# Attention beside routed experts on one core: the output bias in eight group additions ahead of the returns, and a small memset behind each return

## What is computed

```
xn  = layernorm(x)
att = linear attention with 16 heads and exp features(xn) @ w_out + b_out
gates = sinkhorn((xn @ router_w.T + router_b) / temperature), 3 iterations
top 2 experts of 8 for each token, their gates normalised
y   = sum over the 2 experts of gate * ((relu(xn @ wg) * (xn @ wp)) @ wo)
out = x + att + (xn + y)
```

## Time and profile before

| | |
|---|---|
| runs | 329.74 us median of 3 (328.19 to 330.65) |
| profiled execution | 327.3 us, its span 325.5 us |
| busy share of the span | PE 84%, DVE 68%, ACT 49%, POOL 73% |
| mean granted TensorE clock | 0.909 of full speed |
| scatter on POOL | until 164.9 us |
| return on POOL | 177.6 to 301.3 us |
| combination and stores | from 302.3 us to the end |

### The profile page before, as it was taken

How to read it: one execution, slowest core, us unless ns; L and a number is a source line. 1 busy time by engine, 2 the same in 40 slices (tenths; PEclk the granted TensorE clock), 3 DMA queues, 4 the chain that set the end, 5 groups by cost and what they waited for, 6 DMA issues and landing times.

```text
span 325.5 us, 6627 instructions
## 1 busy us (share of the span) xinstructions
PE 274.7 (84%) x2044; PEld 257.5 (79%) x2044; DVE 222.9 (68%) x523; ACT 160.3 (49%) x365; POOL 237.6 (73%) x388
## 2 busy tenths in 40 slices
PE   5996878799999999999699999999999999850020
PEld 4896777689999999999599999999999999850010
DVE  4948889668888778888855777777777774500173
ACT  2774562134555555455346677777777775210000
POOL 5899520757888888888611688888888888888381
PEclk9998996589999999999979999999999999885555
DMA  7974000551111111111142598898888841111694
GB/s 236 339 272 164 4 0 0 167 191 45 47 50 52 45 49 46 47 50 51 36 110 61 166 244 245 244 256 251 245 246 248 251 134 48 42 49 40 226 383 174
DMA packets 32462, 45.22 MB, mean 139 GB/s; under 512 B 5328, under 2 KB 21200, under 8 KB 32432
## 3 DMA queue, kind: packets, MB, share of 16 engines
q1 hardware_dynamic: 26592, 33.83, 34.1%
q0 software_dynamic: 4544, 9.84, 9.0%
q10 hardware_dynamic: 1296, 1.20, 1.1%
HBM read 27.17 MB, written 17.68 MB: 138 GB/s over the span
## 4 chain that ended last, share of the span: by engine, by line
PE 49%; POOL 23%; DVE 12%; DMA 6%; issue 5%; ACT 2%; SPq 1%; ACTq 0%; POOLq 0%; DVEq 0%
POOL rows_y L541 17%; PE bank L642 7%; PE bank L666 6%; POOL acc L496 5%; PE bank L618 4%; PE bank L619 4%; PE bank L620 4%; PE bank L656 4%; PE bank L795 3%; DMA xn<-rows_y 2%; PE bank L591 2%; PE bank L783 2%; PE bank L574 2%; PE bank L784 2%; PE bank L785 2%
## 5 line engine op out<-in xcount | busy, mean ns | idle before, releaser
L541 POOL DMA_INDIRECT rows_y<-xn,row_i x78 | 80.5, 1032 | 28.2 <-ACT xn L969 15.1
L532 POOL DMA_INDIRECT slots_x<-xn,slot_i x64 | 63.9, 999 | 29.4 <-DVE slot_i L1195 10.1
L871 ACT ACTIVATE feat<-z_sb 128x512 f32<-128x512 f32 x64 | 39.9, 631 | 65.7 <-DVE z_sb L1065 65.7
L1058 DVE TENSOR_REDUCE neg_max<-bank 128x16 f32<-128x512 f32 x64 | 42.7, 684 | 19.8 <-PE bank L620 19.8
L783 PE MATMUL bank<-xT_high,w_high 128*128 128x256 f32 x156 | 47.3, 303 | 0.5 <-issue 0.5
L785 PE MATMUL bank<-xT_high,w_low 128*128 128x256 f32 x156 | 44.0, 282 | 0.0
L784 PE MATMUL bank<-xT_low,w_high 128*128 128x256 f32 x156 | 44.0, 282 | 0.0
L1065 DVE TENSOR_TENSOR z_sb<-bank,neg_max 128x512 f32<-128x512 f32 x64 | 42.6, 684 | 0.5
L795 PE MATMUL bank<-w_tile,hidden 128*128 128x128 f32 x312 | 41.0, 275 | 0.0
L642 PEld LDWEIGHTS bank<-v_aug,feat 128*128 128x128 f32 x256 | 31.5, 200 | 8.8 <-issue 7.4
L795 PEld LDWEIGHTS bank<-w_tile,hidden 128*128 128x128 f32 x312 | 38.2, 192 | 0.1
(11 more groups left out here) (145 smaller groups left out, 562.5 us busy)
## 6 DMA issues: line engine op xcount, KB each, us to landing
w_tile<-w_expert_dram SPq DMA_DIRECT2D x39, 384.0 KB
slots_x<-w_tile SPq DMA_DIRECT2D x39, 144.0 KB, 2.2
x_tile<-slots_x SPq DMA_DIRECT2D x39, 130.0 KB
acc<-x_dram SPq DMA_DIRECT2D x8, 256.0 KB, 5.3
xn<-rows_y SPq DMA_DIRECT2D x8, 256.0 KB, 5.8
w_tile<-rows_y SPq DMA_DIRECT2D x8, 256.0 KB, 6.5
rows_y<-xn,row_i POOLq DMA_INDIRECT x78, 3.7
slots_x<-xn,slot_i POOLq DMA_INDIRECT x64, 2.3
```

The costliest lines, as they stand in the source:

```text
L532: pool.indirect_dma_start(slots_x, bass.IndirectOffsetOnAxis(slot_i[k][:, i:i + 1], 0), xn[:, j, :], None).then_inc(scattered[n % FLIGHT], 16)
L541: pool.indirect_dma_start(rows_y, bass.IndirectOffsetOnAxis(row_i[:, k, t:t + 1], 0), y_tile(k, t), None)\
L871: act.activation(feat[par][n][:, :], z_sb[n][:, :], ACT.Exp).then_inc(feat_ready, 1)
L1058: dve.tensor_reduce(neg_max[n][:, :], args(n), AX_X, ALU.max, negate=True).then_inc(z_negmax, 1)
```

## The change

`add_bias` now takes a whole group of four tiles (128 x 512 elements) in one POOL instruction, with the bias repeated over the four tiles. The eight of them stand between the last scatter and the first return. Group g waits until the projections of its tiles are in `acc`, for groups 6 and 7 until 13 projections are. In `send_rows` there is no addition any more; behind each of the 78 return DMAs stands a memset of one column of `gap`, which is twice as wide now. DVE waits once for all eight groups, ahead of `add_projection(13)`; its later waits for the bias are gone. The depths of the expert pipeline (`LOOP`, `UP`, `YR`) stay as they are.

```
-        gap = sb("gap", [P, SLOT_TILES])
+        gap = sb("gap", [P, 2 * SLOT_TILES])
...
-            def add_bias(n):
-
-                j, cols = half_tile((n + 4 * (EARLY - 1)) % (2 * NT))
-                pool.tensor_tensor(acc[:, j, cols], acc[:, j, cols], b_out_sb[:, cols], ALU.add).then_inc(bias_added, 1)
+            def add_bias(g):
+
+                tiles = acc[:, g * GROUP:(g + 1) * GROUP, :]
+                pool.tensor_tensor(tiles, tiles, over_tiles(b_out_sb, GROUP), ALU.add).then_inc(bias_added, 1)
...
                 for t in range(2):
                     pool.indirect_dma_start(rows_y, bass.IndirectOffsetOnAxis(row_i[:, k, t:t + 1], 0), y_tile(k, t), None)\
                         .then_inc(y_sent[k % YR], 16)
-                    n = 2 * k + t
-                    for piece in range(n * NT // SLOT_TILES, (n + 1) * NT // SLOT_TILES):
-                        add_bias(piece)
-                pool.memset(gap[:, k:k + 1], 0.0)
+                    pool.memset(gap[:, 2 * k + t:2 * k + t + 1], 0.0)
 
             pool.wait_ge(base_added, 2 * NT)
+            for g in range(NG):
+                pool.wait_ge(acc_added, min(GROUP // 2 * (g + 1), EARLY - 1))
+                add_bias(g)
             pool.wait_ge(acc_added, EARLY - 1)
             for k in range(SLOT_TILES):
                 send_rows(k)
 
-            pool.wait_ge(bias_added, 2 * NT)
+            pool.wait_ge(bias_added, NG)
...
                 dve.wait_ge(base_added, 4 * b + 4)
-                if late(b, EARLY - 1):
-                    dve.wait_ge(bias_added, 2 * NT - 4 * (EARLY - 1))
+                if b == EARLY - 1:
+                    dve.wait_ge(bias_added, NG)
...
                 step(b, b // 2, b % 2, front=b + 1 < NB)
-            dve.wait_ge(bias_added, 2 * NT)
             combine_group(0)
```

## The result

The changed kernel took 335.75 us (median of 4 runs, 332.7 to 337.32), the kernel before 328.97 beside it (327.89 to 330.65). The ratio is 1.019, 95% interval 1.010 to 1.0281: slower, by something between 1% and 3%, where I had forecast 312 us and a range up to 320. The profiled execution took 337.32 us, its span 335.5.

A forecast was written before the change was run, and what follows sets the result against it. POOL's returns were taken as the bound: from 182.41, 96.75 of distances and 2.6 of collisions, plus 0.3 and 25.55 to the end, gave 307.65, taken as 308.0; with run overheads 312 us, range 308 to 320.

The forecast's parts named there:

- What bounded the kernel: End of the chain: 84 us in a row on POOL's returns, each microsecond off coming off the end until DVE's 287.8.
- The additions and memsets: POOL's return: without additions 75 distances of 1.29 us make 96.75; 39 new memsets cost nothing, 4.3 us if uncovered.
- Collisions: POOL's returns held up by DVE's `w_low`: 6.1 us before, taken as 2.6 after, between 0 and 6.1.
- the second rival: Returns lock onto DVE's `w_low`: 15 us of collisions in place of 2.6, 324 us; chance 8%.
- The group additions: Eight on POOL before the first return: 12 us hidden in 12.74 idle; disturbing DVE's `row_i` costs 0.3, bounds 0 to 1.3.
- The rule on the shared port: Whoever starts first holds the port for the whole instruction; DVE's wait beside group additions could be 1.26 to 1.4 us.
- What is late next: Expert loop with faster returns: about 8 GB/s more DMA traffic, little room for row loads, so the loop may end later.
- x: How much later the expert loop ends: taken as 2 us, between 0 and 6.
- the sum: End of kernel: 307.65 by POOL, 307.64 by DVE, taken as 308.0 for the span, 17.5 us below 325.5.
- the landing of the row loads: Expert loop: landing 0.4 us or more longer makes loads the pace, loop 6 to 10 us later, up to 320; 12%.
- The rival "slower": Expert loop: row loads land after over 5.5 us in place of 4.5, loop 25 us later, 335 us; chance 4%.

The follow-up runs named there:

- third group: On one chip beside the kernel before: changed kernel unedited 305.88 us, with one memset a return pair 304.77, with a 128 x 256 memset behind each return 321.23.
- fast chips: Chips on which the changed kernel and its close relatives took some 306 us, where others gave 332 to 337 us.
- first group: Changed kernel with an addition behind each return 331.27 us, a wide memset instead 321.81, one memset a pair 306.07; kernel before with a memset behind every return 326.59.
- fourth group: Changed kernel unedited 306.1 us; with 128 x 256 memsets behind each return 321.83, a third of weights loaded 305.01, two such memsets behind each pair 342.93.
- slow kind: Chips, or jobs, in which the changed kernel and its close relatives took 332 to 337 us in place of some 306.
- two slow jobs: The result's job (changed kernel, 335.75 us) and a job of four edits to its return memsets (none, one a pair, counted, 128 wide), 331.79 to 336.47 us.
- the bare one: Changed kernel with no memset at all in the return: 336.47 us in one job, 306.05 us in another.

## Why the prediction was wrong

**What bounded the kernel: right.** The 84 us on POOL were the bound, and where nothing else goes wrong each microsecond off the return comes off the end, within a microsecond or two (the table). With the changed kernel this has come to its limit, as forecast: there DVE's late attention ends no earlier than the first plane lands.

**The additions and memsets: right.** The changed kernel on the chip of the third group needs 97.0 us from its second pair (183.33) to its last return (280.36); the forecast was 96.75 + 2.6 = 99.4. 70 of its 75 distances are 1.26 to 1.28 us, where I took 1.29; that is most of the difference. A memset behind every return costs nothing: with it, with one a pair and with none the time is 305.9, 306.1 or 304.8, and 306.1 on the fast chips.

**Collisions: fewer than taken.** One return there takes longer than the others, 1.28 us, and their mean is 0.965. The other four of the five longer distances (1.37 to 2.01 us) hold no long return. All five together give 1.9 us, against the 2.6 that I allowed. And in the kernel before it is 11 returns that take 1.22 to 1.47 us, not the 12 that I counted; they give 3.8 us. What the prediction says of them holds in each case: all 11 start while DVE's `w_low` runs and end 0.86 us after it ends. The lock that the second rival feared was seen as well, though not in the changed kernel: with the addition behind each return (first group) 9 returns in a row, one in every second slot tile from 220.9 to 261.5 us, start just behind the start of a `w_low` and take 1.48 to 1.50 us.

```profile
L541 POOL DMA_INDIRECT rows_y<-xn,row_i x78 | 75.3, 965 | 22.7 <-issue 15.7
```

**The group additions: hidden, as forecast,** 9.93 us in a gap of 12.7 where I took 12. The effect on DVE was there: the first two `row_i` take 0.62 and 0.99 us beside them, 0.15 otherwise:

```profile
172.83 0.62 DVE L1274 TENSOR_TENSOR row_i<-x_tile,spare_row 128x2 int32<-128x2 f32 x1
173.37 0.41 DVE L1262 TENSOR_TENSOR xT_low<-bank,xT_high 128x256 fp32r<-128x256 f32 x1
173.71 0.99 DVE L1274 TENSOR_TENSOR row_i<-x_tile,spare_row 128x2 int32<-128x2 f32 x1
```

What reached the loop can't be told from the scatter of its start, 173.7 to 177.6 among all these kernels.

**The rule on the shared port** (Trainium skill, SBUF — State Buffer, "SBUF: two separate sides") fits these two rows: the wait is up to most of one group addition. It did not decide the time.

**The step that failed is "What is late next".** I took x, by how much the expert loop ends later, as 2 us between 0 and 6. On the chips of the third and fourth group that was right: the loop took 96.7 and 97.4 us in place of 96.1 and ended 1.5 and 2.8 us later. In the fourth group DVE's late attention ended within a microsecond of the landing of its first plane, as in the sum, in the third 3.3 us after it, at a granted clock of 0.80 in place of 1.00. There the whole gain was 19.4 and 19.1 us, for 17.5 forecast. On the chip of the result x was 31. My only way to a longer loop was the landing of the row loads. The rival "slower", at 4%, gave 335 for x = 25. That it comes near the 335.75 measured is luck: its mechanism, landings of 5.5 us, is not what the trace shows, and the formula holds there only by the two errors that cancel (late attention 6.5 us longer, what follows it 7.6 us shorter). The scaling that stalls does not wait for a load, the DMA engines are less busy than before, and the stall stays after the last load: the timeline of ACT past 297 us, where the last weights and rows had been asked for at 288, still has

```profile
298.50 0.60 ACT L962 ACTIVATE gate_act<-bank 128x512 f32<-128x512 f32 x1 [0.86 <-PE bank L785]
301.42 1.14 ACT L969 ACTIVATE xn<-bank,x_tile 128x128 f32<-128x128 f32 x4 [2.32 <-remote]
```

with the DMA engines 0.14 busy in the stretch 297 to 302 us. I had counted on a cost of closer returns in bytes (8 GB/s more) and in POOL's time, and put that for the counts between engines at nothing; on the slow kind TensorE's counts came up to 3.9 us late at ACT, 23 us in all.

**The cause of the late signals is not settled.** Shown: they are TensorE's counts; they came in the two slow jobs and in none of the others, with the same program; there they came with every program traced, whose returns follow each other every 1.26 to 1.35 us, with eight group additions throughout; the kind of memset, its count and its place don't matter. Argued only, from the times of the kernel before: that it is free of them there, that the distance is what does it, and that about 1.5 us would avoid it. A mean rate, or POOL's keeping up with ACT, fits as well, and so does the place of the bias, since all programs on the slow kind but the kernel before had the group additions; the stalls going on 130 us behind these make the last unlikely. One more rival was not tested. The five traces with late signals, and only they, lack a third of their semaphore records (4107 to 4247, against 6273 to 6451 in all others). That may be a mark of the same trouble, or the recording may have a part in it; every run on record has a measured span and clock, so there is none without the recording to tell. I first read "pattern of the memsets" out of a comparison across two chips; that was my error, and the third group exists because of it.

## What to carry to other kernels

A gain that is read from one engine's queue must be checked against what its faster pace does to the counts of all the others: compare, tile by tile, the end of the producer with the start of a consumer that waits for nothing else. When such a start is late at two engines at once, and the recorded time of the count is late too, it is not the load or the data that is missing. And put the two kernels to be compared on one chip in one job, and the pair on more than one chip before you trust a gain: here the same program was 6% faster than its predecessor on two chips and 2% slower in the job of the result.

## What the runs showed of the hardware

- ACT started 0.04 to 0.1 us after the end of the matmuls whose count it waited for in the kernel before. On the slow kind of chip, in kernels in which POOL issued indirect DMAs every 1.26 to 1.35 us, it started up to 3.9 us after it. Later matmuls of TensorE had started before the count came.
- In the five traces with late signals only TensorE's counts were late; the recorded counts of ACT and DVE came within 0.01 us of their instructions' ends. TensorE's held counts came together: four between 189.28 and 189.48.
- The changed kernel took 305.88 and 306.1 us on two chips and 335.75 in the job of the result; the bare one 306.05 and 336.47 on two chips. The medians of the kernel before varied by only about 1% (325.19 to 329.16).
- The late attention of the changed kernel took 22.1 us behind the loop at a mean granted clock of 0.61 (the result), 17.2 at 0.80 (third group) and 14.4 at 1.00 (fourth group).
- A DMA of POOL takes the same 0.96 us with a memset of one column behind it or with nothing, and the next starts 1.26 to 1.27 later in both.
